# Talking-heads attention on one core: the mixing product on 125 rows and 120 columns in place of two row halves

## The reference, cut to what matters

```python
attn = jnp.einsum('bhnd,bhmd->bhnm', q, k) * scale
attn = jnp.einsum('gh,bhnm->bgnm', th1_w, attn) + th1_b[None, :, None, None]
attn = jax.nn.softmax(attn, axis=-1)
attn = jnp.einsum('gh,bhnm->bgnm', th2_w, attn) + th2_b[None, :, None, None]
out = jnp.einsum('bhnm,bhmd->bhnd', attn, v)
```

## Time and profile before

| | us |
|---|---|
| median of 2 runs | 5546.43 |
| their range | 5540.65 to 5552.21 |
| the profiled execution | 5556.62 |
| its span, from the first to the last instruction | 5554.9 |

### The profile page before, as it was taken

The page is one execution under the profiler, slowest core; times in us unless marked ns, Lnnn a source line. Parts: engine busy times, 40 slices in busy tenths (PEclk is TensorE's granted clock), DMA queues, the critical chain, the costliest instruction groups (busy, mean ns, idle before and its releaser), DMA issues. The chain is left out here.

```text
span 5554.9 us, 138694 instructions
## 1 busy us (share of the span) xinstructions
PE 4892.5 (88%) x55425; PEld 3959.4 (71%) x55426; DVE 2510.0 (45%) x7454; ACT 2083.1 (38%) x4629; POOL 1586.8 (29%) x2584
## 2 busy tenths in 40 slices
PE   1389999899977999999999999999999959969950
PEld 0246677566656888888888888888888848857740
DVE  2456555466644555555545555455554421112221
ACT  0034444255543444444444444444444412212210
POOL 0010000266653333333333333233333212111133
PEclk8589999699998999999999999999999979989975
DMA  2011211000000000000000000000000033131112
GB/s 64 0 23 25 47 38 26 5 1 1 1 6 3 5 5 8 8 8 8 2 8 8 8 9 2 8 8 8 8 5 6 8 34 20 13 106 34 34 36 79
DMA packets 74475, 101.52 MB, mean 18 GB/s; under 512 B 14570, under 2 KB 62053, under 8 KB 73910
## 3 DMA queue, kind: packets, MB, share of 16 engines
q1 hardware_dynamic: 61556, 76.99, 6.6%
q0 software_dynamic: 10128, 14.45, 1.0%
q10 hardware_dynamic: 2226, 1.95, 0.2%
HBM read 58.67 MB, written 34.65 MB: 17 GB/s over the span
## 5 line engine op out<-in xcount | busy, mean ns | idle before, releaser
L2063 PE MATMUL PS<-th_kT,th_qg 64*125 64x274 f32 x10560 | 1417.7, 400 | 0.0
L1792 POOL TENSOR_TENSOR th_qg<-th_qT,th_th 128x180 f32<-128x180 f32 x1760 | 846.1, 503 | 1686.3 <-PE PS L2063 1672.1
L1971 ACT ACTIVATE th_P<-PS 110x600 f32<-110x600 f32 x880 | 647.2, 735 | 1233.7 <-PE PS L2050 1233.7
L2050 PEld LDWEIGHTS PS<-th_mixn,th_P 61*110 61x110 f32 x17600 | 981.5, 173 | 100.8 <-issue 23.3
L2063 PEld LDWEIGHTS PS<-th_kT,th_qg 64*125 64x125 f32 x10560 | 942.1, 185 | 139.6 <-POOL th_qg L1792 0.2
L1899 DVE TENSOR_REDUCE th_nmx<-PS 125x1 f32<-125x548 f32 x880 | 641.0, 728 | 880.8 <-PE PS L2063 880.8
L2050 PE MATMUL PS<-th_mixn,th_P 61*110 61x60 f32 x17600 | 976.6, 254 | 1.8 <-ACT th_P L1971 1.8
L1981 ACT ACTIVATE th_P<-PS,th_nb 125x548 f32<-125x548 f32 x880 | 621.2, 706 | 106.8 <-DVE th_nb L1902 106.8
L1200 POOL TENSOR_SCALAR ga_P<-ga_P,ga_rw 110x110 f32<-110x110 f32 (+4 forms) x240 | 264.9, 1115 | 203.9 <-DVE ga_rw L1360 203.9
L2082 PE MATMUL PS<-th_P,th_v 110*32 110x90 f32 (+1 forms) x11520 | 265.4, 253 | 1.3 <-ACT th_P L1971 0.8
L2082 PEld LDWEIGHTS PS<-th_P,th_v 110*32 110x32 f32 x11520 | 244.7, 115 | 27.5 <-issue 26.6
(11 more groups left out here) (320 smaller groups left out, 6576.7 us busy)
## 6 DMA issues: line engine op xcount, KB each, us to landing
pf_xT<-pf_spill SPq DMA_DIRECT2D x32, 412.5 KB, 5.4
ce_w<-in_L_ffn_W SPq DMA_DIRECT2D x18, 576.0 KB
ex_outputs<-ce_y SPq DMA_DIRECT2D x77, 96.0 KB, 1.6
pf_spill<-pf_xT SPq DMA_DIRECT2D x16, 412.5 KB, 3.7
ex_tokens<-th_xn SPq DMA_DIRECT2D x16, 412.5 KB
ex_turned<-th_rT SPq DMA_DIRECT2D x16, 412.5 KB, 3.1
ea_x<-ex_turned SPq DMA_DIRECT2D x16, 412.5 KB, 11.0
out_h<-X SPq DMA_DIRECT2D x4, 1320.0 KB
```

Source lines behind the costliest of these rows:

```text
L1792: ins = pool.tensor_tensor(qg[:, m % SB, :, 64 * s:64 * s + HQ].rearrange("p c (h n) -> p c h n", n=QH), qT[:, im % 2, :, at + s * QH:at + ...
L1971: act.activation(P2[:, :, :, at * QT:(at + 1) * QT].rearrange("p t h (s n) -> p s (t h) n", s=2), PS[0:R, MB:MB + 2, 0:VO].rearrange("p s ...
L2050: ins = pe.matmul(PS[0:R, MB + s, t * HQ:(t + 1) * HQ], P[a, p, t * R:(t + 1) * R], mixn[a, p], start=True, stop=True)
L2063: ins = pe.matmul(PS[0:MR, bank + a, 0:HK], qg[s, p, c, 0:MR], kT[s, im % 2, c, :], start=c == 0, stop=c == NC - 1)
```

## The change

All ten queries of a tile are mixed by one product. The mixing matrix gets 120 columns: 12 heads x (2 halves x 5 queries). It is zero where a row of one half meets a column of the other. The stationary operand is then a block of 110 keys on all 125 rows, so a tile has five matmuls of 120 columns. Three blocks of 120 columns go to bank 6 and two to bank 7, and ACT copies each bank with an instruction of its own (360 and 240 columns). The scaled matrix that DVE makes has 120 columns where it had 60. The setup builds the larger matrix once.

```diff
-    mix = keep("mix", [MR, H, QH])
+    mix = keep("mix", [MR, H, QT])
@@ (setup)
-        d3 = ctx.enter_context(nc.sbuf_tensor("th_d3", [MR, H + 1, QH], F32))
-        d2 = ctx.enter_context(nc.sbuf_tensor("th_d2", [MR, QH], F32))
+        d3 = ctx.enter_context(nc.sbuf_tensor("th_d3", [MR, 2, H + 1, QH], F32))
+        d2 = ctx.enter_context(nc.sbuf_tensor("th_d2", [MR, 2, QH], F32))
@@
-                dve.tensor_tensor(mix[:], th2[:].unsqueeze(2).broadcast_to([MR, H, QH]),
-                                  d2[:].unsqueeze(1).broadcast_to([MR, H, QH]), ALU.mult).then_inc(cp, 1)
+                dve.tensor_tensor(mix[:], th2[:].unsqueeze(2).broadcast_to([MR, H, QT]),
+                                  d2[:].rearrange("p s n -> p (s n)").unsqueeze(1).broadcast_to([MR, H, QT]), ALU.mult).then_inc(cp, 1)
@@ (buffers)
-        mixn = sb("mixn", [MR, SB, H, QH])
+        mixn = sb("mixn", [MR, SB, H, QT])
@@ (ACT)
-                        act.activation(P2[:, :, :, at * QT:(at + 1) * QT].rearrange("p t h (s n) -> p s (t h) n", s=2),
-                                       PS[0:R, MB:MB + 2, 0:VO].rearrange("p s (x n) -> p s x n", n=QH), ACT.Copy).then_inc(p2_in, 1)
+                        for t0, t1 in ((0, 3), (3, T)):
+                            ins = act.activation(P2[:, t0:t1, :, at * QT:(at + 1) * QT],
+                                                 PS[0:R, MB + t0 // 3, 0:(t1 - t0) * H * QT].rearrange("p (t h n) -> p t h n", h=H, n=QT), ACT.Copy)
+                        ins.then_inc(p2_in, 1)
@@ (PE)
                         for t in range(T):
-                            for s in range(2):
-                                a = slice(64 * s, 64 * s + HQ + 1)
-                                ins = pe.matmul(PS[0:R, MB + s, t * HQ:(t + 1) * HQ], P[a, p, t * R:(t + 1) * R], mixn[a, p],
-                                                start=True, stop=True)
+                            ins = pe.matmul(PS[0:R, MB + t // 3, t % 3 * H * QT:(t % 3 + 1) * H * QT], P[:, p, t * R:(t + 1) * R], mixn[:, p],
+                                            start=True, stop=True)
```

More of the change, by code:

```diff
@@ L1665, in _ @@
                 pool.wait_ge(z, 2)
-                pool.affine_select(out=d3[:, 0:H, :], in_=d3[:, 0:H, :], compare_op=ALU.not_equal, fill=1.0, base=0,
+                pool.affine_select(out=d3[:, 0, 0:H, :], in_=d3[:, 0, 0:H, :], compare_op=ALU.not_equal, fill=1.0, base=0,
                                    pattern=[[-QH, H], [-1, QH]], channel_multiplier=1).then_inc(z, 1)
@@ L1672, in _ @@
                 pool.wait_ge(z, 4)
-                pool.affine_select(out=d3[:, 0:H, :], in_=d3[:, 0:H, :], compare_op=ALU.not_equal, fill=1.0, base=-64,
+                pool.affine_select(out=d3[:, 1, 0:H, :], in_=d3[:, 1, 0:H, :], compare_op=ALU.not_equal, fill=1.0, base=-64,
                                    pattern=[[-QH, H], [-1, QH]], channel_multiplier=1).then_inc(z, 1)
@@ L1676, in _ @@
                 for s in range(2):
-                    pool.affine_select(out=d3[:, H, :], in_=d3[:, H, :], compare_op=ALU.not_equal, fill=float(N),
+                    pool.affine_select(out=d3[:, s, H, :], in_=d3[:, s, H, :], compare_op=ALU.not_equal, fill=float(N),
                                        base=-(64 * s + HQ), pattern=[[0, QH]], channel_multiplier=1).then_inc(z, 1)
@@ L1685, in _ @@
                 dve.wait_ge(z, 7)
-                dve.tensor_reduce(d2[:], d3[:].rearrange("p h n -> p n h"), AX.X, ALU.add).then_inc(cp, 1)
+                dve.tensor_reduce(d2[:], d3[:].rearrange("p s h n -> p s n h"), AX.X, ALU.add).then_inc(cp, 1)
                 dve.tensor_scalar(th1[:], th1[:], HD ** -0.5, None, ALU.mult).then_inc(cp, 1)
                 dve.wait_ge(cp, 2)
-                dve.tensor_tensor(mix[:], th2[:].unsqueeze(2).broadcast_to([MR, H, QH]),
-                                  d2[:].unsqueeze(1).broadcast_to([MR, H, QH]), ALU.mult).then_inc(cp, 1)
+                dve.tensor_tensor(mix[:], th2[:].unsqueeze(2).broadcast_to([MR, H, QT]),
+                                  d2[:].rearrange("p s n -> p (s n)").unsqueeze(1).broadcast_to([MR, H, QT]), ALU.mult).then_inc(cp, 1)
     with ExitStack() as ctx:
```

## The result

| | before | changed |
|---|---|---|
| median, us | 5546.43 | 5879.16 |
| range of 2 runs, us | 5540.65 to 5552.21 | 5873.21 to 5885.11 |
| span of the profiled execution, us | 5554.9 | 5883.4 |
| PE busy, us | 4892.5 | 5224.7 |
| matmul records | 55425 | 46625 |

The ratio is 1.058 (95% interval 1.050 to 1.067): the kernel became 333 us slower, with 8800 matmul records fewer. The forecast was 5901. Every execution compared in this document ran undisturbed but one of the ten of the run with the change's work on ACT and DVE alone, which took 7541.7 us at a granted clock of 0.64 and isn't in that run's ratio.

What follows compares the result with a forecast made beforehand. PE was taken to bound the talking-heads stage, its mixing bound by weight loads. Record cost 97, plain-step switches 239 and half trips 19 gave +355 us on 5546: 5901 us, range 5800 to 6010.

Steps and rivals of the forecast that it cites:

- The bound: Talking-heads stage: it lasts as long as PE's instructions; PE busy all but 0.45 of 2434 us.
- Record cost: Mixing product: ten full-height records at 103 ns take 1.03 us against 0.92, +0.11 us per tile.
- The floor for the load: Mixing: a 110-column weight load takes 92 ns, paired on row halves, just hidden under a 120-column full-height stream.
- Switches: Between mixing and scores: going to full height and back adds 0.34 us in 704 plain steps, 0.17 in 112 others.
- two rows of transposes: Steps with two and eight full-height transposes between scores and mixing: they leave 0.31 us for a round trip of shape.
- Steps with other work: Steps with items after the scores: no added trip in 4 per image, half a trip (0.17 us) in 7.
- Eviction and scaling: ACT's two evictions take 0.49 and 0.37 us, +0.13 together; DVE's scaling grows 0.06 to 0.07; both hidden under PE.
- The room for the eviction: ACT before PE's next mixing: some 1.1 us available, 0.86 plus the pass-on fits with about 0.2 to spare.
- No change: Rival, PE's shape switches cost nothing: only +97 us remains, 5643 us; 7%.
- Faster: Rival, a mixing record costs 46 ns whatever its height: 5399 us with the switches; 3%.
- much slower: Rival, weight load not hidden at full height: 195 ns per mixing record, 6710 us; 4%.
- the round trip: PE going from row halves to full height and back: 0.34 us each, ends 0.31 and 0.41.

Runs made afterwards that it cites:

- two mixed-shape kernels: Kernel before with its score product put at full height, mixing left on row halves: 5765.2 us, ratio 1.0386; and the changed kernel itself, scores on halves: 5879.16 us.
- 60-column run: Changed kernel with only 60 of the 120 columns in each full-height mixing matmul: 5779.5 us, ratio 1.0404 against the kernel before.
- split order on row halves: Kernel before with each step's matmuls reordered: three fifths of mixing, two thirds of scores, rest of mixing, last third: 6059.6 us, ratio 1.0899.

## Why the prediction was right, point by point

**The bound.** PE is the only engine that sets the step, before and after. The run with the other engines' work alone gave 1.0002.

**Record cost.** Predicted 103 ns a record and +0.11 us a tile. The step fell by 0.10 when the stream was cut under the load, and the mixing is 1.02 with all at full height against 0.92. The first row is 1.09 us to the start of the next, and not 1.10, so 91 ns a record; nothing hangs on it. The floor for the load was right from both sides: 60 columns at full height don't go below it, and 100 columns on halves don't rise above it.

**Switches.** Predicted +0.34 a plain step; measured 0.42 - 0.10 = 0.32. For 704 plain steps the change is 704 x 0.42 = 296 us. The prediction's two rows of transposes gave 0.31 and the output product 0.36. It chose nearer to the second; the first was nearer.

**Steps with other work.** Predicted +0.11 where only full-height items stand, and +0.28 where value products do, 38 us in all. The first kind measures 6.69 against 6.63 us, +0.06: the mixing after the items goes from 1.01 to 1.12, but the items ahead of it are followed by no change of shape any more (the 24 records take 3.99 where they took 4.08), and the scores ahead of those take 1.58 for 1.54. For the second kind the lines of the kernel before, timeline of PE, are these:

```profile
2386.86 1.61 PE L2063 MATMUL PS<-th_kT,th_qg 64*125 64x274 f32 x12
2388.40 2.87 PE L2030 MATMUL PS<-th_wv,th_xT 96*110 96x192 f32 x16
2391.20 2.78 PE L2082 MATMUL PS<-th_P,th_v 110*32 110x100 f32 x120
2393.91 1.18 PE L2050 MATMUL PS<-th_mixn,th_P 61*110 61x60 f32 x20
2394.92 1.38 PE L2063 MATMUL PS<-th_kT,th_qg 64*125 64x274 f32 x10
```

From score start to score start that is 8.06 us, and 2482.29 - 2473.99 = 8.30 in the changed kernel: +0.24. The 16 steps of the 64-column key product behave like these, as predicted: in the timelines 2347.99 - 2343.44 = 4.55 us before and 2046.88 - 2042.09 = 4.79 in the changed kernel. Together 64 x 0.06 + 112 x 0.24 = 31 us.

**Eviction and scaling.** The two evictions take 0.48 and 0.37 us (predicted 0.49 and 0.37), and as one starts before the other's end they span 0.74 together. The scaling takes 0.29 us, a little under the predicted 0.31. The room for the eviction was under-sized: it starts 0.11 us after the scores, ends 0.74 later, and the next mixing starts at 1.58 or so, so 0.74 us are to spare where the prediction had 0.2. The scores start at 2471.19, and the other lines are:

```profile
2471.25 0.28 DVE L1916 TENSOR_SCALAR th_mixn<-th_mix,th_rs 125x120 f32<-125x120 f32 x1
2471.30 0.74 ACT L1972 ACTIVATE th_P<-PS 110x360 f32<-110x360 f32 x2 [1.36 <-PE PS L2050]
2472.78 1.09 PEld L2050 LDWEIGHTS PS<-th_mixn,th_P 125*110 125x110 f32 x10 [0.36 <-issue]
```

**The rivals.** "No change" fell with the two mixed-shape kernels (2.69 and 2.79 against 2.37 and 2.42). "Faster" and "much slower" fell with the 60-column run: a record is 91 or 92 ns, neither 46 (half as long as its load) nor 92 + 51 = 143 (load and stream of 60 columns one after the other). The Trainium skill's statement (TensorE: Matmul & The Clock Gate, Part 3) that loads overlap only with matmuls of other row groups doesn't hold for these records: at full height 120-column records with 110-column loads take 102 ns. The background weight buffer that the same part names would allow it; no run here shows the buffer itself. What the Trainium skill says of a drain on a change of tiling mode (TensorEngine Tiling (Array Packing), Key Properties) agrees with the 0.19 to 0.20 us measured for a change.

**The sum.** 296 + 31 = 327 us by the steps, and the spans differ by 5883.4 - 5554.9 = 328.5; the medians by 333. The forecast was 355. Of the 28 us between, 21 are the 0.03 us by which a plain step was over-sized (2.82 for 2.79), and 7 the other steps. No step of the argument failed; the one term that was too large is the round trip, 0.34 for 0.32 (and the stream, 0.11 for 0.10).

What stays open: what the 0.20 us consist of. The loads of the next group start with its first matmul, and not ahead of it, so a load (0.09 to 0.10) is exposed; the rest may be the running out of the last matmuls. No run here separates the two. The split order on row halves points the same way without any change of shape: the piece before the wait takes 2474.15 - 2473.04 = 1.11 us, 0.46 of it stream and 0.40 the wait, so running empty and starting again costs some 0.25 beyond the wait. No version that beats the kernel before came out of this: a true score product on 192 channels at full height would stream more than the halves do (two chunks of 96 rows by two key halves, 8 records of 232 ns, 1.86 us for 1.39), more than the round trips of the items would give back. That is worked out, not run.

## What to carry to other kernels

Before replacing two products on row halves by one at full height, look at what stands on either side of it in PE's order: if the neighbours stay on halves, each step pays two changes of shape, here 0.32 us net, and the halved count of instructions pays for none of it. Find out what bounds a record, its weight load or its stream, from a row where the other is small; records bound by paired loads gain nothing from being merged. And when reordering PE's work for an experiment, check first which eviction the order was covering.

## What the runs showed of the hardware that was not expected

Each change between row halves and full height cost close to 0.20 us (0.78 for four), and they add: one round trip in a score product cost 0.39, a second one in the changed kernel 0.40. Groups of equal shape at full height followed each other at no cost (2.42 us for 1.02 + 1.40), while on row halves a step of the two is 0.06 longer than its loads and stream (2.37 against 0.92 + 1.39). At full height an f32 record with 60 columns takes 91 or 92 ns, as long as one with 34 columns and a load as wide; on halves a step is 2.37 us with 60 columns and with 100.
